# Context attention scores of a two-layer transformer block: one 96-row product of 78 columns for each head in place of three block-diagonal products of 308

## The reference, cut to what matters

```python
# _mha(_ln(y), memory, ...), for each batch and head; hd = 32, 16 heads
q = (xq @ wq.T + bq)            # 2048 x 32 a head
k = (memory @ wk.T + bk)        #   77 x 32 a head
v = (memory @ wv.T + bv)
scores = q @ k.T / sqrt(hd) + bias
attn = softmax(scores, axis=-1)
out = (attn @ v) @ w_out.T + b_out
y = y + out
```

## Time and profile before

| | us |
|---|---|
| median of 3 runs | 2832.87 (2831.19 to 2835.78) |
| the profiled execution | 2835.19 |
| its span, first to last instruction | 2833.4 |
| PE busy | 2710.7 (96%) |
| DVE busy | 1606.8 (57%) |
| ACT busy | 1237.7 (44%) |
| mean granted TensorE clock | 0.98 of full speed |

### The profile page before, as it was taken

The page is one execution under the profiler, slowest core; times in us unless marked ns, Lnnn a source line. Parts: engine busy times, 40 slices in busy tenths (PEclk is TensorE's granted clock), DMA queues, the critical chain, the costliest instruction groups (busy, mean ns, idle before and its releaser), DMA issues. The chain is left out here.

```text
span 2833.4 us, 39987 instructions
## 1 busy us (share of the span) xinstructions
PE 2710.7 (96%) x12704; PEld 1795.0 (63%) x12704; DVE 1606.8 (57%) x3852; ACT 1237.7 (44%) x2624; POOL 408.7 (14%) x494
## 2 busy tenths in 40 slices
PE   7999969999999999999999989889989999999998
PEld 6788844444444444444444478667768888888887
DVE  5554357777778777777777388467643222122211
ACT  2322113555555555555555534388843223332232
POOL 4000012000000000000000322088547000000000
PEclk9999978999999999999999999999999999999999
DMA  7656563222222222222222388455431000000000
GB/s 220 225 182 208 179 152 84 68 68 68 68 69 69 69 69 67 57 63 61 62 61 53 103 221 252 174 172 179 142 127 42 30 30 30 22 9 30 30 16 15
DMA packets 137813, 272.39 MB, mean 96 GB/s; under 512 B 24773, under 2 KB 54725, under 8 KB 132362
## 3 DMA queue, kind: packets, MB, share of 16 engines
q1 hardware_dynamic: 132394, 254.57, 31.2%
q0 software_dynamic: 5216, 15.33, 1.9%
HBM read 175.44 MB, written 99.98 MB: 97 GB/s over the span
## 5 line engine op out<-in xcount | busy, mean ns | idle before, releaser
L1157 ACT ACTIVATE sa_pr<-sa_st 128x512 f32<-128x512 f32 (+3 forms) x1280 | 610.4, 532 | 557.6 <-DVE sa_st L1220 318.1
L1125 PE MATMUL sa_ov<-sa_pr,sa_v 128*33 128x512 f32 (+3 forms) x2560 | 533.8, 538 | 0.0
L1206 DVE TENSOR_REDUCE sa_part<-sa_mp 128x1 f32<-128x512 f32 (+3 forms) x768 | 411.0, 581 | 113.0 <-PE sa_mp L1106 113.0
L1116 PE MATMUL sa_st<-sa_q,sa_k 97*128 97x512 f32 (+3 forms) x1280 | 440.6, 413 | 16.2 <-ACT sa_pr L1157 12.8
L1116 PEld LDWEIGHTS sa_st<-sa_q,sa_k 97*128 97x128 f32 x1280 | 216.4, 189 | 316.4 <-ACT sa_pr L1157 209.7
L1106 PE MATMUL sa_mp<-sa_k,sa_q 96*128 96x512 f32 (+3 forms) x1280 | 372.7, 385 | 26.2 <-DVE sa_mp L1184 20.0
L1858 PE MATMUL ff_o<-ff_w,ca_q 128*128 128x512 f32 x1536 | 373.4, 392 | 3.8 <-DVE ca_q L1911 3.8
L1203 DVE CUSTOM_DVE_ANT_0 sa_mp<-sa_mp,sa_ub 128x512 f32<-128x512 f32 (+3 forms) x512 | 317.2, 662 | 77.5 <-PE sa_mp L1106 66.7
L147 PE MATMUL ff_f<-ff_ln_hi,ff_w 128*128 128x512 f32 x1024 | 337.2, 390 | 2.9 <-DVE ff_ln_lo L272 2.9
L1858 PEld LDWEIGHTS ff_o<-ff_w,ca_q 128*128 128x128 f32 x1536 | 285.7, 188 | 65.6 <-DVE ca_q L1911 3.7
L1911 DVE TENSOR_TENSOR ca_q<-ca_v,ca_q 128x512 fp32r<-128x512 f32 x128 | 97.7, 763 | 379.9 <-ACT ca_q L1894 379.9
(11 more groups left out here) (198 smaller groups left out, 3302.0 us busy)
## 6 DMA issues: line engine op xcount, KB each, us to landing
sa_q<-scratch_q SPq DMA_DIRECT2D x96, 256.0 KB, 7.9
sa_k<-scratch_k SPq DMA_DIRECT2D x96, 256.0 KB, 8.7
scratch_q<-qkv_qst SPq DMA_DIRECT2D x32, 512.0 KB, 7.0
scratch_k<-qkv_qst SPq DMA_DIRECT2D x32, 512.0 KB, 5.7
scratch_q<-sao_qst SPq DMA_DIRECT2D x32, 512.0 KB, 4.5
ca_q<-scratch_q SPq DMA_DIRECT2D x32, 512.0 KB, 4.3
scratch_v<-qkv_vst SPq DMA_DIRECT2D x8, 1056.0 KB, 5.2
sa_v<-scratch_v SPq DMA_DIRECT2D x16, 528.0 KB, 12.8
```

What stands on the lines that cost most here:

```text
L1116: pe.matmul(st[bank(u, h)][:, 0:w], ks[n.par][:, h, kb * P:(kb + 1) * P], qs[n.par][:, h, g * GW + c0:(g + 1) * GW], start=True, stop=True ...
L1125: last = pe.matmul(ov[64 * h:64 * h + VW, c0:GW], vs[n.par][:, kb, h, :], pr[:, u % 4, h, 0:GW - c0], start=(u in opens), stop=(u in ends))
L1157: act.activation(pr[:, u % 4, h, 0:w], st[bank(u, h)][:, 0:w], ACT.Exp, scale=SCALE).then_inc(s["exp"], 1)
L1206: dve.tensor_reduce(to, tile, AX_X, ALU.max).then_inc(s["red"], 1)
```

## The change

A query tile now has 96 rows for each head: its high part, its high part again, and its low part. The keys stand in the same 96 rows as high, low, high. One product of these 96 rows sums all three terms. The four heads of a tile are four products, each with its own weights (96 x 128 of the query) and 78 columns (77 and one more, `SW`) of one head's keys, in place of three products of 308 columns with weights of 128 x 128.

To build the 96 rows, each query chunk is loaded with three transfers of 32 partitions (the high part twice), 256 KB each, in place of one of 512 KB over 128 partitions. So are the keys: 3 transfers in place of 8. The buffers of a query chunk are twice as long, so the memory is laid out anew: a `Pair` of buffers lives through all blocks and holds what other blocks had of their own (staging of the last group in `project`, splits of `feed_forward`, residual tiles), and six of the sixteen pieces of one weight matrix of `feed_forward` go where keys and queries had been. One staging buffer of `attention_out` is now the self attention's output buffer, and ACT waits at the start of that block until it is stored.

```diff
+FF_REST = 6
+SW = S + S % 2
+class Pair:
+    def __init__(self, k):
+        self.q = k.sb("sa_q0", [P, 2, T], F32R)
+        self.k = k.sb("sa_k0", [P, 2, T], F32R)
+        self.v = k.sb("sa_v", [P, 2 * KB * 2 * VW])
+        self.flat_q, self.flat_k = (t[:].rearrange("p h t -> p (h t)") for t in (self.q, self.k))
+    def half(self, i, of_q):
+        flat = self.flat_q if of_q else self.flat_k
+        return flat[:, KC * GW * i:KC * GW * (i + 1)].rearrange("p (c t) -> p c t", c=KC)
+Q_PARTS, K_PARTS = (0, 0, 1), (0, 1, 0)
+def cross_keys(dr, b, j):
+    return dr["ck"].ap()[b, K_PARTS[j]].rearrange("(h d) t -> d h t", d=HD)
+def load_query(sp, dr, q, tile, sem):
+    g, m = q // KC, q % KC
+    for j in range(3):
+        rows = dr["qk"][0][Q_PARTS[j], m * P:(m + 1) * P, g * GW:(g + 1) * GW].rearrange("(h d) t -> d h t", d=HD)
+        sp.dma_start(raw(tile[j * HD:(j + 1) * HD]), rows).then_inc(sem, 16)
...
 # project
-        qst = k.sb("qkv_qst", [P, 4, 2, GW], F32R)
-        vst = k.sb("qkv_vst", [P, 2, NPAIR, TT, 2, VW])
+        qst = [t.rearrange("p (n l t) -> p n l t", n=4, l=2)
+               for t in (pair.flat_q, x[:].rearrange("p s i f -> p (s i f)").bitcast(F32R))]
+        qst = [qst[g == NG - 1] for g in range(NG)]
+        vst = [k.sb("qkv_vst", [P, NPAIR, TT, 2, VW])[:],
+               pair.v[:].rearrange("p (a k h e) -> p a k h e", a=NPAIR, k=TT, h=2)]
...
 # self_attention, POOL: the keys of batch 0
-            for hl in range(2):
-                for j in range(HC):
-                    pool.dma_start(raw(key0[j * HD:(j + 1) * HD, hl, :, j * S:(j + 1) * S]),
-                                   dr["ck"].ap()[0, hl].rearrange("(c j p) t -> j p c t", j=HC, p=HD)[j])\
-                        .then_inc(s["early"], 16)
+            for j in range(3):
+                pool.dma_start(raw(key0[j * HD:(j + 1) * HD, :, 0:S]), cross_keys(dr, 0, j)).then_inc(s["early"], 16)
...
 # attention_out, SP in the last group
                     for m in range(2):
                         sp.wait_ge(sq[f"q{m}"], 16)
-                        sp.dma_start(raw(early[2][:, m]), query_chunk(dr, m)).then_inc(sq["ahead"], 16)
+                        load_query(sp, dr, m, early[2][:, m], sq["ahead"])
...
 # attention_out, staging and ACT
-            qst = k.sb(f"{name}o_qst", [P, KC, 2, GW], F32R)
+            qst = k.sb(f"{name}o_qst", [P, KC - 1, 2, GW], F32R)
+            qst = [qst[:, m] for m in range(KC - 1)] + [first.osb[:].bitcast(F32R)]
...
+            for i in range(2):
+                act.wait_ge(first.st[f"st{i}"], 16 * NPAIR * B * GB)
...
 # cross_attention
-    W = HC * S
+    W = HC * SW
-        qb = [early[2][:, 0], early[2][:, 1], k.sb("ca_q2", [P, 2, GW], F32R)[:]]
+        qb = [early[2][:, 0], early[2][:, 1], k.sb("ca_q2", [P, HC, GW], F32R)[:]]
-        kd = [early[0], k.sb("ca_k1", [P, 2, KC, W], F32R)]
+        kd = [early[0], k.sb("ca_k1", [P, H, SW], F32R)]
...
-                sp.dma_start(raw(qb[q % QB]), query_chunk(dr, q)).then_inc(s[f"q{q % QB}"], 16)
+                load_query(sp, dr, q, qb[q % QB], s[f"q{q % QB}"])
...
-                for x, (a, c) in enumerate(((0, 0), (0, 1), (1, 0))):
-                    last = pe.matmul(sps[n % 3][:, 0:W], qb[q % QB][:, a, t], kd[b][:, c, m, :],
-                                     start=(x == 0), stop=(x == 2))
+                for j in range(HC):
+                    last = pe.matmul(sps[n % 3][:, j * SW:(j + 1) * SW], qb[q % QB][0:3 * HD, j, t],
+                                     kd[b][0:3 * HD, m * HC + j, :], start=True, stop=True)
...
-                    last = act.activation(pq_rows[r][:, j, :], sps[n % 3][:, j * S:(j + 1) * S], ACT.Exp,
+                    last = act.activation(pq_rows[r][:, j, :], sps[n % 3][:, j * SW:j * SW + S], ACT.Exp,
...
-                tile = sps[n % 3][:, 0:W].rearrange("p (h k) -> p h k", h=HC)
+                tile = sps[n % 3][:, 0:W].rearrange("p (h k) -> p h k", h=HC)[:, :, 0:S]
...
 # feed_forward: splits of the norm in the pair's buffers, one weight matrix in two places
         norm = Norm(k, "ff_ln", lncols, ident, norm_room(room[5]),
-                    room[0][:].rearrange("p l c t -> p (l c t)")[:, 0:KC * GW].rearrange("p (c t) -> p c t", c=KC))
+                    [(pair.half(i, True), pair.half(i, False)) for i in range(2)], room[7])
```

More of the change, by code:

```diff
@@ L755, in _ @@
             dve.memset(ones[:], 1.0 / D).then_inc(en["ones"], 1)
-            dve.memset(vst[:, :, :, :, :, HD:VW].rearrange("p a b c d e -> p (a b c d e)"), 1.0).then_inc(s["one"], 1)
+            for t in vst:
+                dve.memset(t[:, :, :, :, HD:VW].rearrange("p a k h e -> p (a k h e)"), 1.0).then_inc(s["one"], 1)
             for i in range(TT):
@@ L774, in _ @@
             dve.wait_ge(s["cols"], 48)
-            dve.wait_ge(s["one"], 1)
+            dve.wait_ge(s["one"], 2)
             for i in range(NG):
@@ L883, in __init__ @@
         self.st = {f"st{i}": k.sem(f"sa_st{i}") for i in range(2)}
-        self.split = [[t[:].rearrange("p h t -> p (h t)")[:, KC * GW * i:KC * GW * (i + 1)].rearrange("p (c t) -> p c t", c=KC)
-                       for i in range(2)] for t in (self.k, self.q)]
+        self.split = [[pair.half(i, of_q) for i in range(2)] for of_q in (False, True)]
 def load_outputs(sp, dr, t, cols, sem):
@@ L908, in batch_inverses, with self_attention @@
     return dr["inv"].ap()[:, b * T:(b + 1) * T].rearrange("h (e t) -> h e t", e=P // H)
-def self_attention(k, name, dr, ident, weights, early, first):
+def self_attention(k, name, dr, ident, weights, early, first, pair):
     nc = k.nc
@@ L955, in self_attention @@
     with k:
[L956 to L957 removed]
+        qs = [pair.q[0:QK], k.sb(f"{name}_q1", [QK, 2, T], F32R)[:]]
+        ks = [pair.k[0:QK], k.sb(f"{name}_k1", [QK, 2, T], F32R)[:]]
         sums = k.sb(f"{name}_sums", [P, H * T // P])
         inv = k.sb(f"{name}_inv", [P, H * T // P])
[L960 removed]
+        vs = [pair.v[:, KB * 2 * VW * i:KB * 2 * VW * (i + 1)].rearrange("p (k h e) -> p k h e", k=KB, h=2) for i in range(2)]
         tb = [k.sb(f"{name}_tb{i}", [P, 2, 2 * P]) for i in range(2)]
@@ L1270, in cross_attention @@
         pt = k.sb("ca_pt", [S, 2, HC, GW])
-        oh = k.sb("ca_oh", [P, 2, KC, GW], F32R)
-        ol = k.sb("ca_ol", [P, 2, KC, GW], F32R)
-        y = k.sb("ca_y", [P, YB, D])
+        oh, ol = ([pair.half(i, of_q) for i in range(2)] for of_q in (True, False))
+        y = pair.v[:, 0:YB * D].rearrange("p (e f) -> p e f", e=YB)
         brow = k.sb("ca_brow", [P, D])
@@ L1542, in _ @@
             residual(NE - 1)
-def query_chunk(dr, q):
+def load_query(sp, dr, q, tile, sem):
     g, m = q // KC, q % KC
-    return dr["qk"][0][:, m * P:(m + 1) * P, g * GW:(g + 1) * GW].rearrange("l p t -> p l t")
+    for j in range(3):
+        rows = dr["qk"][0][Q_PARTS[j], m * P:(m + 1) * P, g * GW:(g + 1) * GW].rearrange("(h d) t -> d h t", d=HD)
+        sp.dma_start(raw(tile[j * HD:(j + 1) * HD]), rows).then_inc(sem, 16)
 def norm_room(t):
@@ L1560, in near_heads, with attention_out @@
     return dr["ca_U"].ap()[i * P:(i + 1) * P, first:last, :]
-def attention_out(k, name, io, dr, ident, w, src, dst, wq, early, room, first):
+def attention_out(k, name, io, dr, ident, w, src, dst, wq, early, room, first, pair):
     nc = k.nc
@@ L1650, in _ @@
                 sp.wait_ge(sq[f"q{m}"], 16 * NG)
-            sp.wait_ge(sq["ahead"], 16 * 4)
+            sp.wait_ge(sq["ahead"], 16 * 8)
         @block.gpsimd
```

126 lines of the change are left out of this document (62 added, 64 removed).

## The result

The changed kernel takes 2850.58 us (median of five runs, 2844.01 to 2859.87), the kernel before 2832.87. The ratio is 1.0055, 95% interval 1.0042 to 1.0069: slower by 12 to 20 us. Forecast were 2836.6 us and a range up to 2842.5. The direction was one that the prediction gave 0.29; the size is that of a rival with a chance of 0.13, in which the clock stays low through the slots without projection (2849).

A forecast was written before the change was run, and what follows sets the result against it. PE was taken to bound the projection slots, ACT those before, the DMA queue the end of attention_out and the block's start. Products -1.0, loads ahead +3.2, block start +1.5 make +3.7 on 2832.87: 2836.6 us, range 2831 to 2842.5.

The forecast's parts named there:

- The direction: Sign for the whole kernel: same 0.66, slower (over 2838.5 us) 0.29, faster 0.05.
- a rival with a chance of 0.13: Slots before the projection: clock stays low longer, slots 8 to 9 us in place of 6; 2841.6 to 2849 us; chance 0.13.
- Before 1884.5: Slots without projection: ACT is the limit, narrow products for few tiles make no difference of weight; taken as 0.
- Query loads ahead, +3.2: End of attention_out: larger query loads into 32 partitions delay the last store and the barrier; +3.2 us, bounds 0 to +5.4.
- Start of the block, +1.5: Start of the changed block: larger query chunk 2 delays the near bias behind it, and DVE waits; +1.5 us.
- Products, -1.0: PE-bound slots: eight load-bound products replace six column-bound ones, -0.02 us for each of 48 half slots; -1.0, upper end +2.9.
- Costed at nothing, query loads in the slots: The 32 slots: larger query chunks fit, on DMA engines 49% busy and issued about two slots ahead; no cost.
- narrow products are not slow: Rival, score products: 78 columns cost what 308 do, +15 us, about 2851 us; chance 0.05.
- loads do not come closer than 0.11: Rival, PE-bound slots: weight loads come closer, at 81 ns, -0.25 us a half slot, about 2825.6 us; chance 0.04.
- the DMA time does show: Rival, transfers: the DMA time does not show, only -1.0 and up to +1 us remain, about 2832.4 us; chance 0.17.

The follow-up runs named there:

- four_narrow_early: Kernel before, chunks 0 to 6: only the high x high product, its 308 columns done as four products with four weight loads; 2848.02 us, ratio 1.0038.
- one_term_early: Kernel before, chunks 0 to 6: only the high x high product, one of 308 columns a tile in place of three; 2835.62 us, ratio 0.9995.
- wide_all: Changed kernel with overlapping score products of 312, 234, 156 and 78 columns in all 32 chunks, same weight loads and output; 2846.25 us, ratio 1.0037.
- wide_early: Changed kernel with overlapping score products of 312, 234, 156 and 78 columns in chunks 0 to 6, same weight loads and output; 2843.84 us, ratio 1.0022.
- early_loads: Changed kernel with the bias pieces and the loads of query chunks 0 and 1 issued two groups earlier in attention_out; 2847.76 us, ratio 1.0038.
- full_partitions: Changed kernel with the six query loads ahead in attention_out spread over 128 partitions in place of 32, same bytes; 2847.75 us, ratio 1.0044.
- near_first: Changed kernel with the near bias issued ahead of query chunk 2 at the start of cross_attention; 2846.68 us, ratio 1.0035.
- three_edits: Changed kernel with the edits of wide_early, early_loads and near_first together, same output; 2836.45 us, ratio 0.9995.

## Why the prediction was wrong

The step that failed is *"Before 1884.5"*: "At clock 0.5 the loads are 0.21 us apart, thus 0.84 for four, against 3 x 0.26 us for 308 columns at 1.2 GHz: no difference of weight for the few tiles made so." The comparison of a tile was nearly right (0.229 x 4 = 0.92 us against 0.77). "The few tiles" was the error. It took the time at which the clock came back from the trace of before and held it fixed, though the same edit changes what PE does until then. In the profiled execution all the tiles up to the first projection were made at half clock, and `four_narrow_early` against `one_term_early` shows that more loads over the same columns do this: 57.0 us in place of 46.3, and 12 us by the medians. The price stood in the rival: "8 to 9" us a slot "in place of 6, some 2.5 more"; measured 8.67 against 6.1. Its whole case, 2849, is 1.6 us from the median, which is partly luck: that sum still has -1.0 for the products, where +2.0 was measured, and +3.2 for the loads ahead, where the traces have 2.2 to 2.7. I gave it 0.13 with the argument that transposes and values keep PE busy; the windows show PE busy and the clock low.

The other steps:

- *Query loads ahead, +3.2*: right in kind, somewhat too large: +2.7 in PE's wait in this pair of traces, 2.2 on average over the traces. Its split was between volume and partitions; both are real, volume the larger.
- *Start of the block, +1.5*: right, +1.1 in DVE's wait; taking the bias first gave back 2.7.
- *Products, -1.0*: wrong sign, inside its bounds. The load pitch was right (0.112 against 0.11), and so was the projection's product 0.92 us after the first score load (0.93 forecast), but what it gains is given back in its own pair, 0.71 us in place of 0.63. 0.041 x 48 = +2.0, near the upper end of +2.9.
- *Costed at nothing, query loads in the slots*: right for this kernel; that the DMA engines are 49% busy did not measure the margin.
- *Rivals*: narrow products are not slow (`wide_all`), loads do not come closer than 0.11, the DMA time does show.

The sum in the profiled execution is 13 (clock: 12.1 less the bias's 1.1, and 2 in the first projection slot) + 2.7 + 1.1 + 2.0 = 18.8 us; with the 9.4 us that `wide_early` returned over all executions in place of the 13 it is 15.2. The medians say 17.7, the interval 12 to 20.

Two things stay open. The profiled execution held the low clock to the projection, others with the same products climbed back earlier (`early_loads` after 31 us, `full_partitions` with a mean of 0.62 over its 52.8 us); how often the unprofiled executions do either isn't known. Their mean clocks point both ways: two of the five of the changed kernel have 0.977 and 0.978, the values of the profiled `early_loads` (0.977) and not those of a clock that stays low (0.969 to 0.974 in the profiled executions of the changed kernel, `near_first` and `four_narrow_early`). And whether the shorter pause helped `early_loads` to its earlier climb, or chance, isn't separated: `four_narrow_early` had the short pause (7.6 us) and stayed low. Why the clock falls a second time in `three_edits`, `wide_all` and the kernels with one load is open too.

## What to carry to other kernels

When products are cut narrower than their weight loads, price them by loads, not by columns, and do it at both clock levels: here 16 loads a slot at half clock turned an ACT-bound stretch of 6.1 us a slot into a PE-bound one of 8.7. Never take the moment at which the clock returns from the old trace when the edit changes PE's work before it; price the stretch at either clock, and if the new work might hold it down, give that case real weight. Before looking for the next gain on PE, take PE's work away in an experiment and see what it waits for: here the query loads, half as many bytes again in three transfers, stood right behind PE and would have swallowed 24 us (212.1 against 187.8).

## What the runs showed of the hardware

- More columns over the same weight loads made the kernel 9.4 us faster by the medians (780 in place of 312 a tile, for 28 tiles). In its trace the clock came back 19 us after the first score and not only after the projection had begun, 62 us after it.
- A clock that has come back can fall again at once: in `wide_all` it was 1.00 from 1865.3 to 1870.3 and 0.57 on average in the 12 us after, with PE busy 4.81 of 5.00 and 11.02 of 12.00 us.
- PE busy 100% in the records with a granted clock of 0.50 for 40 us (`four_narrow_early`): the busy share does not foretell the clock. What the chip counts, these runs do not tell.
- Weight loads of 128 columns follow each other at 0.112 us at clock 1.0 and 0.229 at 0.5, with 78-column products between them; widening those to 195 columns on average adds 0.008 us a product.
- 1.57 MB into 32 partitions at a time took 7.4 us, over 128 partitions 6.1.
